# Attention over eight images on one core: two batches of work share each tile shape on TensorE, row maxima are turned by halves

## What is computed

```python
hyp_out = _logmap0(_mhsa(_expmap0(hyp_feat), hdn_w_qkv, hdn_b_qkv, hdn_w_o, hdn_b_o))
euc_out = _mhsa(euc_feat, eu_w_qkv, eu_b_qkv, eu_w_o, eu_b_o)
# in _mhsa: t is (B, 1024, 512)
qkv = t @ w_qkv + b_qkv
scores = jnp.einsum('bhnd,bhmd->bhnm', q, k) / jnp.sqrt(jnp.float32(hd))
attn = jax.nn.softmax(scores, axis=-1)
out = jnp.einsum('bhnm,bhmd->bhnd', attn, v)
out = out @ w_o + b_o
```

## Time and profile before

| | us |
|---|---|
| median of 3 runs | 4010.45 |
| lowest and highest | 4008.18, 4010.48 |
| the profiled execution: time | 4012.71 |
| the profiled execution: span of its instructions | 4011.0 |

### The profile page before, as it was taken

One profiled execution on the slowest core, in us unless ns is written; L12 is line 12 of the kernel. 1 busy time (PEld: TensorE's weight loads), 2 busy tenths in 40 slices (PEclk: granted clock), 3 DMA queues, 4 the chain that ended last, 5 costly groups with the idle time before them and its releaser, 6 DMA issues.

```text
span 4011.0 us, 57066 instructions
## 1 busy us (share of the span) xinstructions
PE 3940.3 (98%) x21676; PEld 2383.3 (59%) x21676; DVE 2344.5 (58%) x2553; ACT 1927.8 (48%) x3489; POOL 2658.5 (66%) x1300
## 2 busy tenths in 40 slices
PE   5999999999999999999999999999999999999999
PEld 3556566565655656556565665656656565565655
DVE  5464755647556575565746657465574656736455
ACT  4454534545345453455535545355453545535443
POOL 4584875838668386674867658575585756858468
PEclk9999999999999999999999999999999999999999
DMA  8212031120311203112131121411113111121101
GB/s 283 95 43 95 32 116 59 43 95 32 124 51 46 97 32 126 53 48 85 32 128 60 47 82 32 142 46 56 69 41 133 48 69 53 53 95 43 64 11 64
DMA packets 137548, 293.12 MB, mean 73 GB/s; under 512 B 16704, under 2 KB 28992, under 8 KB 127296
## 3 DMA queue, kind: packets, MB, share of 16 engines
q1 hardware_dynamic: 137280, 289.47, 21.2%
HBM read 239.09 MB, written 50.33 MB: 72 GB/s over the span
## 4 chain that ended last, share of the span: by engine, by line
PE 94%; DVE 2%; DMA 1%; POOL 1%; issue 1%; ACT 0%; SPq 0%; POOLq 0%; DVEq 0%; ACTq 0%
PE aux_ps L1326 32%; PE acc_ps L1439 23%; PE score_ps L1425 22%; PE aux_ps L1375 8%; PE score_ps L1326 4%; PE aux_ps L1453 3%; DVE mxp L1186 1%; PE aux_ps L1385 1%; POOL sums L681 0%; DMA probs<-in_L_conv_eu_w_o_dram 0%; DMA xin<-in_x_dram 0%; DMA w_split<-v_y 0%; PE aux_ps L1341 0%; PE aux_ps L1344 0%; POOL o_t L661 0%
## 5 line engine op out<-in xcount | busy, mean ns | idle before, releaser
L681 POOL TENSOR_TENSOR sums<-sums,probs 128x1024 f32<-128x1024 f32 x765 | 1829.4, 2391 | 737.7 <-ACT probs L860 683.7
L1186 DVE TENSOR_REDUCE mxp<-aux_ps 128x2 f32<-128x1024 f32 x1014 | 1242.1, 1225 | 1300.8 <-PE aux_ps L1375 1293.2
L860 ACT ACTIVATE probs<-score_ps 128x512 f32<-128x512 f32 x2048 | 1058.0, 602 | 659.4 <-PE score_ps L1425 648.2
L1439 PE MATMUL acc_ps<-probs,v_y 128*64 128x512 f32 x4096 | 993.3, 606 | 0.0
L1326 PE MATMUL aux_ps<-xs,w_qk 128*128 128x512 f32 x2976 | 804.9, 408 | 0.0
L1326 PEld LDWEIGHTS aux_ps<-xs,w_qk 128*128 128x128 f32 x2976 | 525.5, 188 | 373.9 <-issue 279.1
L681 POOL TENSOR_TENSOR sums<-probs 128x1024 f32<-128x1024 f32 x128 | 305.2, 2384 | 433.3 <-ACT probs L860 432.6
L1439 PEld LDWEIGHTS acc_ps<-probs,v_y 128*64 128x64 f32 x4096 | 248.5, 136 | 475.6 <-issue 250.4
L1375 PE MATMUL aux_ps<-k_hi,q_hi 64*128 64x512 f32 x2028 | 455.2, 444 | 19.7 <-DVE mxp L1186 16.9
L1248 DVE RECIPROCAL den<-den 128x256 f32<-128x256 f32 (+1 forms) x240 | 443.5, 1848 | 20.3 <-ACT den L871 20.3
L1425 PE MATMUL score_ps<-q_hi,k_hi 64*128 64x512 f32 x2048 | 408.5, 394 | 1.0 <-issue 1.0
(11 more groups left out here) (144 smaller groups left out, 3159.5 us busy)
## 6 DMA issues: line engine op xcount, KB each, us to landing
w_qk<-w_split SPq DMA_DIRECT2D x124, 512.0 KB, 4.2
xin<-in_x_dram SPq DMA_DIRECT2D x232, 256.0 KB, 3.1
w_o<-w_split SPq DMA_DIRECT2D x32, 1024.0 KB, 7.5
w_v<-w_split SPq DMA_DIRECT2D x30, 1024.0 KB, 5.9
v_y<-in_x_dram SPq DMA_DIRECT2D x72, 256.0 KB, 3.0
y<-v_y SPq DMA_DIRECT2D x64, 256.0 KB, 2.0
xin<-y SPq DMA_DIRECT2D x64, 256.0 KB, 2.9
out_dram<-v_y SPq DMA_DIRECT2D x64, 256.0 KB, 6.6
```

The costliest lines, as they stand in the source:

```text
L681: pool.tensor_tensor(sums[h][:, :], a, probs[:, g % SLOTS_P, :], ALU.add).then_inc(c_sum[h].sem, 1)
L860: act.activation(probs[:, n % SLOTS_P, token_half(u % 2)], score_ps[:, u % SCORE_BANKS, :], ACT.Exp, scale=SCALE).then_inc(c_exp.sem, 1)
L1186: dve.tensor_reduce(mxp[:, :, n, h], ps, AX.X, ALU.max).then_inc(c_free["D"].sem, 1)
L1439: last = nc.tensor.matmul(acc_ps[head(j), :], v_y[:, m, head(2 * p + j)], probs[:, n % SLOTS_P, token_half(j)], start=(m == 0), stop=(m == ...
```

## The change

What stood in one batch is now spread over a pair of batches, an even one and the odd one behind it:

- `projections`: a whole projection (12 matmuls) in each even batch, or four `v_tile` in b = 0 and b = 2; none in odd batches.
- `held`: prob_v of the even and of the odd batch (four tiles, 16 records) stand behind the odd batch's scores, with the denominator between them. Where an even batch has no projection (the last half-image from b = 20 on) prob_v follows as it did.
- `neg_rows` by halves: four identity matmuls for the queries of one half, inside an even batch's projection, between its first and last six matmuls (b = 6, 14, 22, 30 for h = 0 and b = 8, 16, 24 and the next b = 0 for h = 1), always in aux_ps bank 1. `combine` is twice as often and half as wide. `q_max` has one buffer. The gate's small matmuls stand in the same place of the projection, in bank 0.
- ScalarE has o_hi, masks and squares ahead of the q_max and denominator copies. Some statistics and squares change batches (STATS_AT, NORM_AT), and SyncE issues the load of w_o behind those of the next input.

```diff
-NEG_AT = -1
+HALF_DONE = (11, 15)
+NEG_AT = (-2, 0)
...
-STATS_AT = {1: (0, 1, 2), 2: (3, 4, 5), 3: (6, 7)}
+STATS_AT = {1: (0,), 2: (1, 2, 3, 4, 5), 3: (6, 7)}
...
-NORM_AT = {0: (0, 1), 1: (2,), 2: (3, 4), 3: (5,), 4: (6, 7)}
+NORM_AT = {0: (0,), 1: (1, 2, 3), 2: (4, 5), 3: (6,), 4: (7,)}
...
+def neg_at(i, t, b):
+    for h in range(2):
+        p, r = divmod(b - NEG_AT[h], 8)
+        if r == 0 and wanted(i, t, p):
+            return p, h
+    return None
...
 def projections(b):
-    out = [("v", m) for m in (2 * b, 2 * b + 1) if m < NT]
+    out = [("v", m) for m in range(2 * b, 2 * b + 4) if b % 2 == 0 and m < NT]
     for p in range(2, PAIRS + 2):
-        for k in range(4):
-            done = min(8 * p + QK_AT[k], BATCHES)
-
-            first = done if (p, k) in ((PAIRS, 0), (PAIRS + 1, 3)) else done - 1
-            out += [("qk", p, k, part) for part in range(2) if b == (first, done)[part]]
+        out += [("qk", p, k) for k in range(4) if b == min(8 * p + QK_AT[k], BATCHES)]
     return out
-def made(b):
-
-    return [f[:3] for f in projections(b) if f[0] == "v" or f[3]]
+def projects(i, t, b):
+    return any(f[0] == "v" or wanted(i, t, f[1]) for f in projections(b))
+def held(i, t, b):
+    if projects(i, t, b - b % 2):
+        return (b - 1, b) if b % 2 else ()
+    return (b - 1, b) if b == BATCHES - 1 else (b - 1,) if b % 2 or not projects(i, t, b - 2) else ()
...
-        if neg_pair(b) is not None and wanted(i, t, neg_pair(b)):
-            out += neg(neg_pair(b))
+        neg = [((t, "neg") + neg_at(i, t, b), "A", (1,))] if b % 2 == 0 and neg_at(i, t, b) else []
+        if b:
+            out += neg
         if t == 0 and b in GATE_BATCH and followed(i):
             out += [((t, GATE_BATCH[b]), "D", (0,))]
-        for f in projections(b):
+        for f in projections(b) if b < BATCHES else ():
             if f[0] == "v":
-                out += [((t,) + f, "A", (LAST_SCORE if f[1] % 2 else 1 if f[1] == 6 else 2,))]
-            elif f[3] and wanted(i, t, f[1]):
-                out += [((t,) + f[:3], "Q", (2,))]
+                out += [((t,) + f, "A", (LAST_SCORE if f[1] % 2 else 2,))]
+                if b == 0 and f[1] == 0:
+                    out += neg
+            elif wanted(i, t, f[1]):
+                out += [((t,) + f, "Q", (2,))]
...
-                    load_wide(w_o, t, 6, c_wo)
                     if t == 0 and followed(i):
                         load_chunks(i, 0, "stats", range(8), next_image)
                         load_gate(i, 0)
                     if t and followed(i):
                         load_chunks(i, 1, "norm", range(4, 8), next_image)
+                    load_wide(w_o, t, 6, c_wo)
...
-                        if phase_at(b, DEN) is not None:
-                            den_copy(phase_at(b, DEN))
-                        if neg_pair(b) is not None and wanted(i, t, neg_pair(b)):
-                            neg_rows(i, t, neg_pair(b))
                         for j in HI_AT.get(b, ()):
                             if wanted(i, t, PAIRS):
                                 operand_hi(i, t, j)
-                        project(b)
                         if phase_at(b, SPLIT) is not None:
                             o_hi(phase_at(b, SPLIT))
                         if t and b == Y_CLAMP:
...
                             step(i, act.activation(sc[:, 2, :], sc[:, 1, :], ACT.Ln, bias=1.0))
                             act.activation(sc[:, 3, :], sc[:, 1, :], ACT.Ln, bias=1.0, scale=-1.0).then_inc(c_ya2d.sem, 1)
                         operand_step(i, t, b)
+                        if b and b % 2 == 0 and neg_at(i, t, b):
+                            neg_rows(i, t, *neg_at(i, t, b))
+                        if phase_at(b, DEN) is not None:
+                            den_copy(phase_at(b, DEN))
+                        project(b)
...
+            def combine(i, t, p, h):
+                aux_read(dve, i, (t, "max", p, HALF_DONE[h]))
                 for j in range(2):
-                    dve.tensor_reduce(mxw[:, HD * j:HD * j + NT], mxp[:, j, :, :], AX.X, ALU.max,
+                    dve.tensor_reduce(mxw[:, h, HD * j:HD * j + NT // 2], mxp[:, j, 4 * h:4 * h + 4, :], AX.X, ALU.max,
                                       negate=True).then_inc(c_mx.sem, 1)
...
+            def neg_rows(i, t, p, h):
+                pe.wait_ge(c_mx.sem, c_mx.at(i, 2 if i is None else 4 * (4 * t + p - 1) + 2 * h + 2))
+                ps = bank_free(pe, i, (t, "neg", p, h))
+                for n in range(4):
+                    last = nc.tensor.matmul(ps[0:HD + 1, n * P:(n + 1) * P], mxw[:, h, n:n + HD + 1], ident[:, :],
+                                            start=True, stop=True)
+                last.then_inc(c_aux.sem, 1)
...
-                            if p:
-                                aux_read(pe, i, (t, "neg", p, 1))
+                        if m == 0:
+                            if p or h:
+                                aux_read(pe, i, (t, "neg", p, h))
                             elif t:
-                                aux_read(pe, i, (0, "neg", PAIRS, 1))
+                                aux_read(pe, i, (0, "neg", PAIRS, 0))
                             else:
                                 pe.wait_ge(c_free["A"].sem, c_free["A"].at(i, 0))
                         pe.wait_ge(c_exp.sem, c_exp.at(i, max(2 * n + 2 - SCORE_BANKS, 0)))
-                        if g % 2 and 1 < g <= NT + 1:
-
-                            aux_read(pe, i, (t, "v", g - 2))
+                        if g in (3, 7):
+                            aux_read(pe, i, (t, "v", g))
...
                     def project(b):
+                        gate = GATE_BATCH[b] if t == 0 and b in GATE_BATCH and followed(i) else None
+                        neg = neg_at(i, t, b) if b % 2 == 0 and b < BATCHES else None
+                        if neg is not None and not projects(i, t, b):
+                            neg_rows(i, t, *neg)
                         for f in projections(b):
                             if f[0] == "v":
                                 v_tile(f[1])
+                                if b == 0 and f[1] == 0:
+                                    neg_rows(i, t, *neg)
                             elif wanted(i, t, f[1]):
-                                qk_tile(i, t, f[1], f[2], (f[3],))
+                                qk_tile(i, t, f[1], f[2], (0,))
+                                if neg is not None:
+                                    neg_rows(i, t, *neg)
+                                if gate is not None:
+                                    gate_tile(i, t, gate)
+                                qk_tile(i, t, f[1], f[2], (1,))
                     for b in range(BATCHES):
                         if b == 0:
...
                         scores(2 * b + 1)
                         if wanted(i, t, p1):
...
-                        if b:
-                            prob_v(2 * b - 2)
-                            prob_v(2 * b - 1)
-                        if phase_at(b, DEN) is not None:
-                            denominator(phase_at(b, DEN))
-                        if neg_pair(b) is not None and wanted(i, t, neg_pair(b)):
-                            neg_rows(i, t, neg_pair(b))
-                        if t == 0 and b in GATE_BATCH and followed(i):
-                            gate_tile(i, t, GATE_BATCH[b])
+                        for bb in held(i, t, b):
+                            prob_v(2 * bb)
+                            prob_v(2 * bb + 1)
+                            if phase_at(b, DEN) is not None and bb == b - 1:
+                                denominator(phase_at(b, DEN))
                         project(b)
-                    prob_v(TILES - 2)
-                    prob_v(TILES - 1)
```

66 lines of the change are left out of this document (26 added, 40 removed).

## The result

| | median us | runs | ratio to before, 95% interval |
|---|---|---|---|
| before | 4009.88 | 4 (4008.18 to 4010.48) | |
| after | 3944.77 | 4 (3944.28 to 3945.25) | 0.9838 [0.9821, 0.9855] |

The change made the kernel 65 us faster, 10 us more than forecast.

A forecast was written before the change was run, and what follows sets the result against it. TensorE, busy for 98% of the span, was taken to bound the kernel. Changes of form -86.9, old waits -5.8 and -1.4, new waits +38 sum to -56 us: 3955 us against the median of 4010.45, 8 in 10 between 3925 and 3988.

The forecast's parts named there:

- What bounds it, and the price of C: TensorE bounds; each stretch of 64-column matmuls (prob_v) costs 0.15 us beyond its records; 250 fewer stretches: -37.5 us.
- The price of Q: Each stretch of whole-array matmuls (projections) costs 0.24 us beyond its matmuls; 233 fewer stretches: -55.9 us.
- neg_rows in 4 and 4: 0: Identity matmuls in projections cost 0.06 us each, in one piece of eight or as 4 and 4: 0 us change.
- New waits of neg_rows: +26: In even batches' projections, neg_rows wait for VectorE's reduction of the second slot: 20.4 plus 5.8, together +26 us.
- b = 20: Second attention's first-slot wait goes, -5.8 us; a new chain of late reduction, reciprocal and slots costs 8 us.
- R behind C +6.5: 64-row slots and scores take 2.53 us behind prob_v instead of 2.50 behind a projection, 217 more times: +6.5 us.
- ScalarE at nothing: ScalarE's new order, with exponentials ready before prob_v and the denominator's copy behind masks, causes no waits: 0 us.
- The denominator in the middle of prob_v: Bank 1 is wanted only 1.8 us after the denominator, behind two prob_v tiles, so its copy costs nothing.
- The cover holds: Rival: VectorE is free when neg_rows comes, new waits are 10 us; 3926, up to 3940 us; chance 0.22.
- The slots turn slower: Rival: even batches' shorter slot gap makes next slots wait; 0.5 us each gives 4029 us; 0.05 shared with the last rival.
- The price is not of the form's change: Rival: stretches' extra time comes with accumulation ends or waits and stays; some 4025 us; 0.05 shared with slower slots.
- the +38: Sum of all new waits, at neg_rows, b = 20 and smaller places: +38 us, between 6 and 90.

The follow-up runs named there:

- the split to four records: The kernel before, with the half projection placed between the two prob_v tiles of a batch, so prob_v runs in stretches of four records: 4222.89 us, ratio 1.053.
- neg_rows stand behind eight: The changed kernel, with neg_rows and the gate's matmuls behind 8 of the projection's 12 matmuls instead of 6: 3936.93 us, ratio 0.9818.
- the kernel with three matmuls: The changed kernel, with neg_rows and the gate's matmuls behind 3 of the projection's 12 matmuls instead of 6: 4048.24 us, ratio 1.0097.
- the experiment with `o_lo`: The changed kernel, with VectorE's o_lo one batch earlier, in odd batches: 3990.5 us, ratio 0.995.

## Why the prediction held, and where it didn't

- **What bounds it, and the price of C.** Right. 0.150 us per stretch came out of after (1.867 + 1.867 - 3.584), of the split to four records, and of two further kernels. C's total was -43.1 for -43.3.
- **The price of Q.** Right for stretches of six and more: two of 1.601 against one of 2.949 give 0.253 for 0.24, 3 us more over 233. It is too high by a fifth for stretches of three. That changes nothing in this sum, since no projection of the kernel is cut so short.
- **neg_rows in 4 and 4: 0.** This step failed. Eight in a piece, with the return to the projection paid by the stretch, are no measure for four in the middle of it. The return costs 0.09 us at 103 stretches and 0.11 at the 16 of b = 0, some 11 us in place of 0.
- **New waits of neg_rows: +26.** Too high, and the two errors cancel. Measured against 3.274, the median where neg_rows stand behind eight, the 103 stretches hold 14.5 us of waits, 3.8 of them once in the start-up, at 86.63. With the way back this makes 26 again, which is luck. The limit was right, as the kernel with three matmuls shows; the reductions' ends were not. At b = 24 I took 2.1 us behind the slot from the trace of before, and it is 1.68 in after, because `o_lo` now starts 0.14 us ahead of GpSimd's line 665 and takes 0.74 us; in before it started 0.40 behind and took 1.45. At b = 16 of the first attention a stretch is 3.85 us long, so it waits 0.58 for 0.75 forecast (0.87 in image 2). At b = 14 of the second, in seven images, it is 0.3 for 0.5, at b = 30 there 0.2 for 0.4, and at b = 24 nothing for 0.45. Whether a VectorE step meets a GpSimd step is decided within 0.3 us, as the experiment with `o_lo` shows; I carried collisions over from one order to another, where they have no reason to stay.
- **b = 20.** The old wait went, as said (-5.8). The new chain I put at 8; it is 3.1 (R of b = 21 takes 0.25 to 0.53 us more than its median, seven times).
- **R behind C +6.5.** The number came true (+6.3) and the reason did not. I expected 2.53 us where R follows C, and those between C and Q take 2.496. The increase is in R between Q and C, 2.518 for 2.497, 250 times, which is 5 us; the rest are waits that came (b = 21) and went (the start-up). What makes these 0.02 us was not tried and stays open.
- **ScalarE at nothing.** Nearly: slots wait 2.9 us for q_max and the denominator. But its cover was looked at only for slots. The v_tile of b = 2 now come four in a row, and the third waits for the copy of the first, which stands behind masks and squares in the second attention: 3.6 us of waits, 5.6 in the stretches. That step was missing.
- **The denominator in the middle of prob_v.** I named it as a cover (1.8 us behind it, two tiles). Two experiments show what it is worth: without it the next slot waits 0.79 us at 110 places. Of all covers costed at nothing this was the one with most behind it.
- **The rivals.** "The cover holds" had 10 us of new waits and the forecast 38. What was waited lies between them: 14.5 at neg_rows, 3 at b = 21, 5.6 at the v_tile. The way back comes on top with 11, and the time lies 5 us above that rival's 3940 and in the lower part of the forecast. "The slots turn slower" is real at a distance of 1.9 us and absent at 3.3. "The price is not of the form's change" is out: kernels with the same matmuls and 276, 303, 511, 526 and 980 stretches of C all show the same 0.150 for each.

Of the 12.5 us by which the profiled execution beat the sum, some 4 stood in the start-up of before: the second slot at 115.03 waited 2.36 us for `mxp`, the longest wait of the earlier trace rows, and R there took 5.44 us. The C behind it took 3.02 for 1.87, at a granted clock of 0.61 (115 to 119 us). Ahead of the slot's reduction VectorE had three statistics steps (L1005), which waited for their input's load until 111.72. In after STATS_AT leaves one of them in that batch, w_o is loaded behind that input, and the step starts at 108.59 without a wait; R takes 2.51 and the clock is 1.00. The forecast had no term for this. By estimate from the terms above, 2 or 3 are new waits, the way back with them, that came out below the +38, and 3 are the price of Q. The rest I can't assign. The other parts of the change (ScalarE's order, the moved statistics, the load of w_o) were not run by themselves, so which of the last two ended this wait isn't shown.
